# Cross attention over the context: 128-row query tiles, block transposes on VectorE, values in four row groups

## The reference, cut to what matters

```python
kv_rope = kv_c * cos[None] + _rotate_half(kv_c) * sin[None]      # 8 x 375 x 128
q_r = jnp.einsum('bshq,hqr->bhsr', q_big, W_qr)
k_r = jnp.einsum('bld,hdr->bhlr', kv_rope, W_kr)
scores = jnp.einsum('bhsr,bhlr->bhsl', q_r, k_r)
attn = jax.nn.softmax(scores, axis=-1)
ctx_c = jnp.einsum('bhsl,bld->bhsd', attn, kv_rope)
```

## Time and profile before

| | us |
|---|---|
| median of 3 runs | 1616.93 |
| profiled execution, its own time | 1617.09 |
| its span | 1615.3 |
| PE busy | 1579.1 (98%) |
| DVE busy | 935.1 (58%) |
| ACT busy | 731.5 (45%) |
| POOL busy | 667.2 (41%) |

### The profile page before, as it was taken

One profiled execution on the slowest core, in us unless ns is written; L12 is line 12 of the kernel. 1 busy time (PEld: TensorE's weight loads), 2 busy tenths in 40 slices (PEclk: granted clock), 3 DMA queues, 4 the chain that ended last, 5 costly groups with the idle time before them and its releaser, 6 DMA issues.

```text
span 1615.3 us, 24574 instructions
## 1 busy us (share of the span) xinstructions
PE 1579.1 (98%) x9834; PEld 1347.0 (83%) x9834; DVE 935.1 (58%) x1525; ACT 731.5 (45%) x1231; POOL 667.2 (41%) x489
## 2 busy tenths in 40 slices
PE   9999999999999999999999999999999999999998
PEld 8997667788899998778889986877778788888887
DVE  6555663366544455587758667355766545554554
ACT  3114564322677765666611157334455333353342
POOL 2974542540498873331228634122424232222221
PEclk9999999999999999999999999999999999999999
DMA  4110003133222007200001100110011111111211
GB/s 171 65 63 19 2 2 130 46 102 128 90 82 66 14 1 273 69 1 1 27 1 66 59 21 14 51 52 21 15 33 52 46 52 64 48 40 46 66 46 46
DMA packets 28580, 88.52 MB, mean 55 GB/s; under 512 B 4154, under 2 KB 4282, under 8 KB 28215
## 3 DMA queue, kind: packets, MB, share of 16 engines
q1 hardware_dynamic: 28468, 86.96, 16.2%
HBM read 85.11 MB, written 1.84 MB: 54 GB/s over the span
## 4 chain that ended last, share of the span: by engine, by line
PE 85%; DVE 6%; ACT 4%; issue 4%; POOL 1%; DMA 0%; SPq 0%; ACTq 0%; DVEq 0%; POOLq 0%
PE PS L263 19%; PE PS L265 19%; PE PS L264 19%; PE PS L268 7%; PE PS L1165 5%; PE PS L1503 3%; PE PS L1520 2%; PE PS L600 2%; PE PS L624 1%; PE PS L992 1%; PE PS L1757 1%; PE PS L1781 1%; PE PS L590 1%; PE PS L608 1%; PE PS L1993 0%
## 5 line engine op out<-in xcount | busy, mean ns | idle before, releaser
L312 POOL TENSOR_TENSOR HL<-stg,HL 128x1024 fp32r<-128x1024 f32 (+2 forms) x109 | 238.5, 2190 | 489.3 <-ACT HL L307 471.2
L263 PE MATMUL PS<-XT,HL 128*128 128x448 f32 x608 | 224.0, 368 | 0.6 <-POOL HL L312 0.6
L265 PE MATMUL PS<-XT,HL 128*128 128x448 f32 x608 | 222.1, 365 | 0.0
L264 PE MATMUL PS<-XT,HL 128*128 128x448 f32 x608 | 222.1, 365 | 0.0
L307 ACT ACTIVATE HL<-stg 128x1024 fp32r<-128x1024 f32 (+2 forms) x110 | 103.6, 943 | 214.4 <-PE PS L265 198.8
L263 PE MATMUL PS<-HL,XT 128*128 128x512 f32 (+1 forms) x380 | 138.0, 363 | 2.3 <-DVE XT L764 2.1
L264 PE MATMUL PS<-HL,XT 128*128 128x512 f32 (+1 forms) x380 | 134.8, 355 | 0.0
L265 PE MATMUL PS<-HL,XT 128*128 128x512 f32 (+1 forms) x380 | 134.8, 355 | 0.0
L263 PEld LDWEIGHTS PS<-XT,HL 128*128 128x128 f32 x608 | 114.2, 188 | 12.6 <-POOL HL L312 1.0
L264 PEld LDWEIGHTS PS<-XT,HL 128*128 128x128 f32 x608 | 114.3, 188 | 9.1
L265 PEld LDWEIGHTS PS<-XT,HL 128*128 128x128 f32 x608 | 114.2, 188 | 9.1
(11 more groups left out here) (323 smaller groups left out, 3807.4 us busy)
## 6 DMA issues: line engine op xcount, KB each, us to landing
stg<-in_wst SPq DMA_DIRECT2D x87, 512.0 KB, 3.3
stg<-in_wst SPq DMA_DIRECT2D x16, 352.0 KB, 3.3
stg<-in_wst SPq DMA_DIRECT2D x16, 320.0 KB, 3.0
wsum<-in_wfc SPq DMA_DIRECT2D x8, 512.0 KB, 3.7
wsum<-in_wpj SPq DMA_DIRECT2D x8, 512.0 KB, 3.6
raw<-in_wfc SPq DMA_DIRECT2D x8, 512.0 KB, 6.4
stg<-in_wst SPq DMA_DIRECT2D x16, 256.0 KB, 2.7
raw<-in_wpj SPq DMA_DIRECT2D x7, 512.0 KB, 6.9
```

The source lines that it names most:

```text
L263: e.matmul(out, lh, rh, start=start, stop=False)
L264: e.matmul(out, lh, rl, start=False, stop=False)
L265: return e.matmul(out, ll, rh, start=False, stop=stop)
L312: e.tensor_tensor(slot(k)[:, 1, 0:n], stg[k % NSTG][:, 0:n], slot(k)[:, 0, 0:n].bitcast(F), A.subtract).then_inc(*done(*low_part(k)))
```

## The change: what it does

In the first cross attention the 896 query rows of half the heads of a batch element (a group, `s`; 16 of them) are cut into 7 tiles of 128 rows instead of 8 of 112. A group still has four units, of 2, 2, 2 and 1 tiles. The PE transposes, the ACT copy `PX` and the DVE copy out are gone. In their place:

- DVE transposes each 128 x 384 tile of shares in 32 x 32 blocks (`e.transpose`, STREAM_TRANSPOSE), 9 columns of zeros padding 375 to 384. The lone tile of the fourth unit is also scaled on DVE (`x_share`), no longer on POOL.
- The values are then products over 32 context rows each: for each of 12 blocks `j`, four fp32 matmuls of 224 columns, one per group of 32 partitions, into banks 4 to 7. They need the values of the batch element four times, once in each 32 partitions (`V4`): SP writes the rotated context to DRAM (`rotated`) and reads it back four times per batch element.
- PE runs the value blocks a group late, in three pieces of four `j`; ACT copies the four banks back to `QO` in one instruction (`out(s)`), ahead of the exponential of its step.
- The weight pieces `ox` 1 and 2 are rounded after the loop, since their buffers hold `TX`; their successors are loaded after the last magnitude.

In the second layer's cross attention, `root2` is issued on ACT ahead of `turned`, and on DVE `stats2(4)`, `ln_lo`, `norm2(3)` ahead of `residual(5)`.

```diff
         def query_parts(e, s, i):
+            q = slot_of(s)[:, (0, 512)[i]:(512, 896)[i]]
...
-                    e.tensor_tensor(Sx[k][:, :, :], Sx[k][:, :, :], rx[:, k, :].unsqueeze(2).to_broadcast([S, 2, L]),
+            return e.tensor_tensor(Sx[k][:, 0:n, 0:L], Sx[k][:, 0:n, 0:L], rx[:, k, 0:n].unsqueeze(2).to_broadcast([P, n, L]), A.mult)
...
+        def x_values(e, s, j0, j1):
+            b = s // 2
+            if j0 == 0:
+                e.wait_ge(*upon("dve_x", "t", 4 * s + 3))
+                e.wait_ge(*upon(f"sp_v4{b % 2}", b, 3))
+                if s:
+                    e.wait_ge(*upon("act_x", "o", s - 1))
...
+            for j in range(j0, j1):
+                for r in range(4):
+                    p = slice(32 * r, 32 * r + 32)
+                    last = e.matmul(PS[:, 4 + r, 0:224], V4[b % 2][p, j, :], TX[s % 2][p, :, 32 * j:32 * j + 32], start=j == 0,
+                                    stop=j == LP // 32 - 1)
...
+                if s > 1 and k < 2:
+                    x_values(e, s - 2, 4 + 4 * k, 8 + 4 * k)
+                if 0 < s <= UX // 4 and k == 3:
+                    x_values(e, s - 1, 0, 4 if s < UX // 4 else 12)
...
+                if k == 2 and s > 1:
+                    out(s - 2)
...
+                if st > 1:
+                    u = st - 2
+                    s = u // 4
+                    if u % 4 == 0 and s > 1:
+                        e.wait_ge(*upon("pe_x", "pv", s - 2))
+                    if u % 4 == 3:
+                        e.wait_ge(*upon("dve_x", "rx", u))
+                        x_share(e, u).then_inc(*done("dve_x", "p", u))
+                        e.wait_ge(*upon("dve_x", "p", u))
+                    else:
+                        e.wait_ge(*upon("pool_x", "p", u))
...
+                    for i, t in enumerate(tiles(u)):
+                        last = e.transpose(TX[s % 2][:, t, :], Sx[u % 4][:, i, :])
...
-                if w > 1:
-                    turned(2 * w - 3)
                 if w == NB:
                     for t in range(3):
                         root2(e, t)
+                if w > 1:
+                    turned(2 * w - 3)
...
                 if w > NB:
+                    stats2(e, 4)
+                    ln_lo(e, "lne", 0, LN_BANK[0])
+                    norm2(e, 3)
+                    ln_lo(e, "lne", 1, LN_BANK[1])
                     residual(e, "o2", 5, O2_BANK[5])
...
+            for c in range(3):
+                e.dma_start(rotated[:, c * 125:c * 125 + 125, :].rearrange("b p d -> p b d"), kvr[:, c, :, :]).then_inc(*landed("sp_rot", c))
...
+            def replicate(b):
+                if b > 1:
+                    e.wait_ge(*upon("pe_x", "pv", 2 * b - 3))
+                for r in range(4):
+                    e.dma_start(V4[b % 2][32 * r:32 * r + 32, :, :],
+                                rotated[b, :, :].rearrange("(j c) d -> c j d", c=32)).then_inc(*landed(f"sp_v4{b % 2}", b, r))
```

More of the change, by code:

```diff
@@ L1126, in x_scores @@
             if u > 1:
                 e.wait_ge(*upon("act_x", "exp", u - 2))
-            for e_ in range(2):
-                i, j = u // 2 % 2, 2 * (u % 2) + e_
-                last = mm3(e, PS[0:S, bank + e_, 0:L + 1], qxh[i][:, j, :], qxl[i][:, j, :], kxh[b % 2][:, :],
+            for t in tiles(u):
+                o = t % 4 * 128
+                last = mm3(e, PS[:, bank + t % 2, 0:L + 1], qxh[i][:, o:o + 128], qxl[i][:, o:o + 128], kxh[b % 2][:, :],
                            kxl[b % 2][:, :], True, True)
@@ L1134, in x_largest @@
         def x_largest(e, u):
-            bank = 2 * (u % 2)
+            bank, n = 2 * (u % 2), len(tiles(u))
             e.wait_ge(*upon("pe_x", "sc", u))
-            e.tensor_reduce(nm[:, u % 4, :], PS[0:S, bank:bank + 2, 0:L], AX.X, A.max,
-                            negate=True).then_inc(*done("dve_x", "nm", u))
+            e.tensor_reduce(nm[:, u % 4, 0:n], PS[:, bank:bank + n, 0:L], AX.X, A.max, negate=True).then_inc(*done("dve_x", "nm", u))
+        def x_values(e, s, j0, j1):
[3 more added lines that the diff above has]
+                e.wait_ge(*upon(f"sp_v4{b % 2}", b, 3))
+                if s:
+                    e.wait_ge(*upon("act_x", "o", s - 1))
+                else:
+                    for half in range(2):
+                        e.wait_ge(*upon("dve_q", "o", 7, half))
+                        e.wait_ge(*upon("act_q", "o", 7, half))
+            for j in range(j0, j1):
[3 more added lines that the diff above has]
+                                    stop=j == LP // 32 - 1)
+            if j1 == LP // 32:
+                last.then_inc(*done("pe_x", "pv", s))
@@ L1156, in pe_x @@
-                if 0 <= st - 4 < UX:
-                    u = st - 4
-                    e.wait_ge(*upon("act_x", "px", u))
-                    if u > 1:
-                        e.wait_ge(*upon("dve_x", "o", u - 2))
-                    else:
-                        e.wait_ge(*upon("pool_ctx", "k", NB - 1))
-                        e.wait_ge(*upon("dve_q", "o", 7, 1))
-                    for c in range(3):
-                        last = e.matmul(PS[:, 6 + u % 2, 0:2 * S], kvr[:, c, u // 8, :], PX[u % 2][:, :, c, :],
-                                        start=c == 0, stop=c == 2)
-                    last.then_inc(*done("pe_x", "pv", u))
+                if s > 1 and k < 2:
+                    x_values(e, s - 2, 4 + 4 * k, 8 + 4 * k)
@@ L1170, in pe_x @@
                     value_of(e, 0)
-                if st == UX + 2:
-                    value_of(e, 1)
-                    e.wait_ge(*upon("act_x", "exp", UX - 1))
-                    e.wait_ge(*upon("act_mag", 15))
-                    e.matmul(PS[:, 2, 0:16], C("ones"), gam[:, :, 8:16], start=True, stop=True).then_inc(*done("pe_thr"))
+            e.wait_ge(*upon("act_x", "exp", UX - 1))
+            value_of(e, 1)
+            e.wait_ge(*upon("act_mag", 15))
+            e.matmul(PS[:, 2, 0:16], C("ones"), gam[:, :, 8:16], start=True, stop=True).then_inc(*done("pe_thr"))
@@ L1186, in act_x @@
                 if st < UX:
-                    k, bank = st % 4, 2 * (st % 2)
+                    bank = 2 * (st % 2)
                     if st > 3:
-                        e.wait_ge(*upon("pe_x", "tr", st - 4))
+                        e.wait_ge(*upon("dve_x", "t", st - 4))
                     e.wait_ge(*upon("dve_x", "nm", st))
-                    for e_ in range(2):
-                        last = e.activation(Sx[k][:, e_, :], PS[0:S, bank + e_, 0:L], ACT.Exp, bias=nm[:, k, e_:e_ + 1],
-                                            scale=1.0, accum_out=sx[:, k, e_:e_ + 1])
+                    for i in range(len(tiles(st))):
+                        last = e.activation(Sx[k][:, i, 0:L], PS[:, bank + i, 0:L], ACT.Exp, bias=nm[:, k, i:i + 1], scale=1.0,
+                                            accum_out=sx[:, k, i:i + 1])
@@ L1210, in dve_x @@
         def dve_x(e):
-            for st in range(UX + 4):
+            for st in range(UX + 2):
                 if 0 < st < UX:
```

169 lines of the change are left out of this document (88 added, 81 removed).

## The result

| | before | after |
|---|---|---|
| median of 4 runs each, us | 1616.82 | 1604.79 (1603.93 to 1606.43) |
| ratio to the kernel before | | 0.9929, 95% interval 0.9918 to 0.9941 |
| span of the profiled execution | 1615.3 | 1602.1 |
| first product of the next stage (PE `PS<-VX,XT`) at | 605.73 | 595.83 |
| first reciprocal of the stage at | 424.09 | 423.83 |

The kernel is faster by 12 us where 24 were forecast. The first attention gave 9.3 in place of 20.7 (25.7 less the 3 and the 2 taken off it): the next stage's first product was due at 585.6 us, came 10.2 later, and 1.0 more was lost right behind it. Ratios and their intervals are of fast runs alone, which leaves out one execution of 4179 us in x14_best and one of 8884 us of the kernel before beside it.

The account below looks back on a forecast made before the run. PE was taken to bound the kernel before, a DVE and POOL chain the new groups. First attention 25.7 us, less 3 and 2, plus 3.4 elsewhere: 24.1 saved, 1593 us; own range 1587 to 1601, 8 in 10 within 1583 to 1609.

Parts of the forecast that it names:

- 25.7 less the 3 and the 2 taken off it: First attention: next stage in step at 580.6 instead of 606.3 us, less 3 for `ox_lo` and 2 for the clock.
- DMA in the head: Start of the first attention: `rotated` and first V4 copies issued before the magnitudes and hidden; magnitudes behind later copies 1 us late.
- 2 us set aside for the clock: First two groups: PE has scores only, its clock falls, and the first value blocks are slow, costing 2 us.
- The period of 9.4: Each first-attention group: DVE and POOL chain of 9.2 us plus small additions gives 9.4; PE's 8.8 fits inside.
- Rival 1: First attention: PE alone is the bound, 8.8 to 8.9 us per group; 8 us less, 1585; 10%.
- `ox_lo` and the tail: Last two groups: `ox_lo` four times in the chain, 3 us; last reciprocal to next stage 15.5 us.
- Rival 4: First attention: DVE transposes at half rate, 0.86 us queued, 0.95 alone; group 11.0 us, total 1619; 5%.
- DVE beside POOL: Each first-attention group: DVE's scaling and POOL's first share collide, so one waits some 0.5 us.
- Rival 2: First attention: DVE and POOL collide worse or POOL passes 9.3; chain 10.3 us, total 1607; 12%.
- rival 3: First attention values: four row groups overlap only in part, 0.25 us a round; PE binds, total 1607; 6%.
- rival 5: Hand-over to the next stage: late `ox` loads and raw weights cost 5 us more than the 0.6 priced; 1598.
- Second edit: Second layer's cross attention, ACT and DVE reordered: earlier last output product and no half clock gain 3.4 us.

Follow-up runs that it names:

- x14_best: Changed kernel with three magnitudes later, last-group split later, magnitude 14 ahead of batch 6's V4 copies, two value blocks per group, writes split 112 and 13: 1587.31 us, ratio 0.9831.
- x5_early: Changed kernel with the `rotated` writes and first eight V4 copies moved between the loads of the stage ahead: 1597.17 us, ratio 0.9885 to the kernel before.
- x13_sixteen: Changed kernel with each 125-partition write to `rotated` split in 112 and 13, queue order kept: 1596.42 us, ratio 0.9880 to the kernel before.
- x11_two_blocks: x8_all with a group's values in two blocks of six steps in place of three of four: 1588.41 us, ratio 0.9826 to the kernel before.
- x9_less_values: x8_all without the second of a group's three value blocks; one execution, mean distance between groups 9.08 us.
- x4_magnitude: Changed kernel with three ACT magnitudes one step later, behind the result copy and the exponential: ratio 0.9919 to the kernel before.
- x7_replicate: Changed kernel with magnitude 14 issued ahead of batch 6's V4 copies; one execution, the 11.68 us distance became 9.60, together 1.2 us won.
- x10_one_row: x8_all with all four matmuls of a value round on the same 32 rows; one execution: 2106.3 us, groups of 40.9 us.
- x12_second_only: Kernel before with only the reordering of ACT and DVE in the second layer's cross attention: 1613.33 us in 11 runs, ratio 0.9979.
- x3_no_second: Changed kernel with the ACT and DVE reordering in the second layer's cross attention undone: ratio 0.9948 to the kernel before, against 0.9929.
- x8_all: Changed kernel with x4_magnitude, x5_early, x7_replicate and a later ACT split of the next stage's first value block together: 1595.30 us, ratio 0.9867 to the kernel before.

## Why the prediction was wrong

The direction was right, and so were the prices of the new layout's parts (rounds, transposes, scores). The size was not, and the engine that binds a group was not the one named. The step that failed is the one on DMA: `rotated` and the first V4 copies "are issued before the magnitudes and hidden", and the magnitudes "can come 1 us late, on ACT, which has slack".

- **DMA in the head, 8.1 us.** It is the largest of the terms behind the 10.2 us by which the next stage's first product came late; 2 us set aside for the clock and 0.8 won in the first distance stand against it, so that 5.3 of the 10.2 are left. I asked whether `rotated` and V4 are in time for the first values, and they were, to 0.3 us. I didn't ask what stands behind them in SyncE's queue, nor how long 1.5 MB in writes of 125 partitions take: I had put no duration on them. They held SyncE from 412.2 to 429, the magnitudes were issued at 433.25 where they could have been at 420 (SyncE does so in x5_early), and ACT has no slack for 7.08 us: an exponential waits behind the magnitude, and all engines behind that. x13_sixteen (the writes' speed) and x5_early (their place) each bring back 7.1 on their own. The clock did fall, but as a part of the stall: 13.65 us at half clock with it, 3.4 us without (x5_early). The row that the 2 us rested on has PE busy for 5.96 of 8 us, a quarter idle and not half.
- **The period of 9.4.** Right by 0.2 in the groups that nothing disturbs, and for another reason. I had the chain over DVE and POOL as the bound at 9.2 and PE at 8.8. By the trace PE's own work is the bound: scores 3.61 and rounds 24 x 0.19 = 4.56 as priced, but going in and out of the row groups costs 0.2 us inside a block and 0.2 at its two ends, 1.2 a group and not 0.6, and a wait of 0.2: 9.6. x11_two_blocks shows that term. x9_less_values shows a loop over the other engines at 9.1, near my 9.2; that it is the same chain isn't shown. So the bound came out near by luck. Rival 1 named the right engine at the wrong size. Cost: 1.3 us in six groups.
- **Magnitudes, 4.8 us.** Three come ahead of the copy to `QO` (2.5 over the forecast; x4_magnitude brings back 1.9); one lands late (11.68, 2.3 over; x7_replicate brings back 1.2 net). The text has "the copy ahead of the exponential delays that by 1 us at a step with 1 us of slack". With a magnitude ahead of both there was no slack.
- **`ox_lo` and the tail.** 3 us were set aside; the last three distances and the tail (16.48 for 15.5) take 2.1 over the bare sum, so 0.9 of the 3 was not needed. No run takes `ox_lo` away by itself. With the first reciprocal 0.3 us sooner the terms give 5.3 + 1.3 + 4.8 - 0.9 - 0.3 = 10.2.
- **DVE's transposes.** 554 ns for 0.55 forecast. Rival 4 fell.
- **DVE beside POOL.** A wait of 0.5 us per group was forecast; three shares are each 71 ns longer than before, and the scaling (531 ns) not at all: 0.2. Rival 2 fell.
- **Row groups.** A factor of 4.0 for the rounds (x10_one_row); rival 3 fell.
- **The next stage** is not in step. PE waits 1.04 us at 597.82 for the split of the second value block, where 0.54 went before: rival 5's place, at a tenth of its price.
- **Second edit.** 3.4 us (x12_second_only), down to the name of the wait that took its place. Taking it away (x3_no_second) brought back the wait of 2.03 us and not the half clock, so that part of the 3.4 hangs on where the clock falls.

The measured 1604.8 us lies outside my own range (1587 to 1601) and inside the wider one (1583 to 1609).

## What to carry to other kernels

Before a transfer is called hidden, give it a duration, and go down the issuing queue behind it: what is issued later, and which engine waits for that in order? Look at the number of partitions of a DMA as at its run length: a DMA share of a third while transfers are waited for is a reason to ask how they are spread, and splitting 125 into 112 and 13 was worth 7 us here. When an engine waits often but briefly, move what it doesn't need next (a magnitude, a split) behind what another engine waits for, whatever its own busy share.

## What the runs showed of the hardware

- Writes of 125 partitions ran at 109 GB/s and a DMA share of 0.36, in runs of 512 bytes and much the same (119) in runs of 4 KB; as 112 and 13 at 264 GB/s and 0.97.
- SyncE's issue of a write of 1000 pieces of 512 bytes took 4.2 us with another such write ahead of it, and 0.34 with none:

```profile
339.44 0.34 SPq L2728 DMA_DIRECT2D rotated<-kvr  x1
...
352.58 0.34 SPq L2728 DMA_DIRECT2D rotated<-kvr  x1
```

  (x5_early). The fourth write, of 36 KB only, took 4.68 us behind the third. So a long issue is here a wait behind the transfers ahead, not the price of its own pieces.
- PE was granted 0.54 of its clock, half of it for most of the time, in a stretch in which its record is busy without a gap, with 32-row matmuls one after the other (x10_one_row):

```profile
600.00:640.00 40.00, 40.00 (x116) 34.20 (x115) 6.93 (x16) 6.27 (x17) 7.79 (x7) 0.54 0.14 36
```

  The same matmuls four at a time had 1.00 (x8_all, 470 to 508.4 us, PE busy 37.62 of 38.40). Why the one fell and the other didn't is in no run.
- A 32 x 32 block transpose of 128 x 384 fp32 on DVE costs 554 ns, and two queued take 1.01 to 1.04.
